# Moving one elementwise product of a selective scan from VectorE to GpSimd, and a sum from TensorE to VectorE

## The reference

```python
uc = silu(conv(u)); dtr, Bt, Ct = split(uc @ x_proj_w.T)
dt = softplus(dtr @ dt_proj_w.T + dt_proj_b)
A = -exp(A_log)
# for every token t, 256 channels, 16 states
h = exp(dt_t[..., None] * A) * h + (dt_t * u_t)[..., None] * B_t[:, None, :]
y = einsum('bdn,bn->bd', h, C_t)
```

## Time and profile before

| what | value |
|---|---|
| time, median of 3 runs | 15182.63 us (15170.1 to 15185.59) |
| profiled execution: its time, its span | 15170.1 us, 15168.0 us |
| mean granted clock of PE | 0.895 of full speed |
| busy: POOL, DVE, PE, ACT | 13633.9, 13545.8, 12942.3, 9178.0 us |

### The profile page before, as it was taken

One profiled execution on the slowest core, in us unless ns is written; L12 is line 12 of the kernel. 1 busy time (PEld: TensorE's weight loads), 2 busy tenths in 40 slices (PEclk: granted clock), 3 DMA queues, 4 the chain that ended last, 5 costly groups with the idle time before them and its releaser, 6 DMA issues.

```text
span 15168.0 us, 190881 instructions
## 1 busy us (share of the span) xinstructions
PE 12942.3 (85%) x60700; PEld 8148.5 (54%) x60700; DVE 13545.8 (89%) x9901; ACT 9178.0 (61%) x10559; POOL 13633.9 (90%) x4234
## 2 busy tenths in 40 slices
PE   7888888888888888888888888888888888888886
PEld 4555555555555555555555555555555555555554
DVE  6988998889898898988899888999989899898996
ACT  4655665656666665665566665665656666566663
POOL 6998999989999898998989998999989899898996
PEclk8998998889899888989889998889988889888997
DMA  4655555555555555555555555555555555555653
GB/s 173 231 214 209 210 217 218 216 206 211 211 220 218 209 213 207 222 219 210 209 210 216 220 212 211 211 212 219 220 205 214 207 219 219 211 211 205 222 221 131
DMA packets 582385, 3200.85 MB, mean 211 GB/s; under 512 B 65875, under 2 KB 65883, under 8 KB 319075
## 3 DMA queue, kind: packets, MB, share of 16 engines
q1 hardware_dynamic: 581346, 3187.69, 56.6%
HBM read 3107.73 MB, written 29.36 MB: 207 GB/s over the span
## 4 chain that ended last, share of the span: by engine, by line
POOL 27%; issue 25%; PE 24%; DVE 17%; ACT 5%; DMA 1%; DVEq 1%; POOLq 0%; ACTq 0%; SPq 0%
POOL ring L884 18%; PE work L1387 13%; POOL ring L867 9%; DVE ring L1375 9%; PE y_acc L1402 6%; DVE slot L1364 4%; PE slot L1387 2%; PE y_acc L1387 2%; ACT ring L1041 1%; ACT L900 1%; DMA b_rows<-cb_rows_scratch 1%; DVE du L1163 1%; ACT stack L940 1%; ACT stack L936 0%; ACT yz L966 0%
## 5 line engine op out<-in xcount | busy, mean ns | idle before, releaser
L884 POOL TENSOR_TENSOR ring<-ring,c_rows 128x2048 f32<-128x2048 f32 x2048 | 9282.8, 4536 | 997.8 <-DVE ring L1375 993.7
L1375 DVE TENSOR_TENSOR_SCAN ring<-ring,slot 128x1024 f32<-128x1024 f32 x2304 | 5263.6, 2285 | 261.6 <-ACT ring L1041 38.2
L1402 PEld LDWEIGHTS y_acc<-wk,ring 128*128 128x128 f32 x32768 | 4252.3, 155 | 1880.0 <-issue 1021.7
L1402 PE MATMUL y_acc<-wk,ring 128*128 128x128 f32 x32768 | 4762.4, 297 | 489.7 <-POOL ring L884 406.8
L867 POOL TENSOR_TENSOR ring<-du,b_rows 128x1024 f32<-128x1024 f32 x1792 | 4236.3, 2365 | 286.6 <-PE y_acc L1402 211.0
L1375 DVE TENSOR_TENSOR_SCAN ring<-slot,ring 128x1024 f32<-128x1024 f32 x1792 | 4074.2, 2274 | 192.1 <-POOL ring L867 116.5
L1041 ACT ACTIVATE slot<-dt,a_neg 128x1024 f32<-128x1024 f32 x1792 | 1997.6, 1115 | 2784.0 <-DVE ring L1375 2777.6
L1364 DVE TENSOR_TENSOR slot<-du,slot 128x1024 f32<-128x1024 f32 x2304 | 2797.4, 1214 | 271.0 <-PE slot L1387 179.7
L1041 ACT ACTIVATE ring<-dt,a_neg 128x1024 f32<-128x1024 f32 x2304 | 2600.9, 1138 | 206.5 <-PE y_acc L1402 157.3
L1387 PE MATMUL work<-h_new,fused 128*128 128x512 f32 x4096 | 2160.0, 638 | 101.7 <-ACT dt L952 53.7
L1387 PE MATMUL slot<-stack,sel 96*128 96x512 bf16 x4608 | 1540.7, 419 | 719.4 <-DVE ring L1375 639.0
(11 more groups left out here) (173 smaller groups left out, 10050.2 us busy)
## 6 DMA issues: line engine op xcount, KB each, us to landing
c_rows<-cb_rows_scratch SPq DMA_DIRECT2D x2048, 1024.0 KB, 4.7
b_rows<-cb_rows_scratch SPq DMA_DIRECT2D x1792, 512.0 KB, 5.5
x_next<-in_x SPq DMA_DIRECT2D x32, 512.0 KB, 5.4
x_new<-x_next SPq DMA_DIRECT2D x32, 512.0 KB, 6.7
h_old<-h_new SPq DMA_DIRECT2D x32, 512.0 KB, 2.9
x_old<-x_new SPq DMA_DIRECT2D x32, 512.0 KB, 6.8
out<-x_old SPq DMA_DIRECT2D x32, 512.0 KB, 2.9
cb_rows_scratch<-stack SPq DMA_DIRECT2D x128, 96.0 KB
```

Of the source, the lines that this page charges most:

```text
L884: pool.tensor_tensor(pair, pair, c_rows[:, k % CB_BUFS, :, :], ALU.mult).then_inc(prod_ready, 1)
L1375: dve.tensor_tensor_scan(slot, a, b, 0.0, MUL, ADD).then_inc(scan_done, 1)
L1402: ins = pe.matmul(chunk(out_t, j), chunk(x, j), kc("ident"), is_transpose=True, start=start and j % (BANK // P) == 0, stop=stop, skip_grou ...
```

## The change

Two things are changed. First, `timestep` is put together in another way. Ln is done in two half tiles, each from `du` into a PSUM bank; DVE adds that bank to `dt` in place (`dt_sum`, one for each half tile); POOL multiplies the whole of `dt` by `u_conv` into `du` (`dt_u`). The identity matmuls and the copy out of PSUM are gone. The waits for the first units of a pass are moved accordingly: the first decay waits for `dt_sum` on DVE, and the first DVE multiplication and the first POOL input of a pass wait for `dt_u` on POOL. Second, `KIND` is "DPDPDPDPDPDPDPDD": the counts are the same, and the two neighbouring "D" units without a "P" between them stand at the pass's end and not in its middle. The planner has costs for the new steps, and `dt_u` is due two units before the pass in place of four.

```diff
-KIND = "DPDPDPDDDPDPDPDP"
+KIND = "DPDPDPDPDPDPDPDD"
...
-    steps += [step(("dt_exp", d, h), "A"), step(("dt_ln", d, h), "A")]
+    steps += [step(("dt_exp", d, h), "A")]
     for c in range(2):
-        b = ("dt2", d, h, c)
-        steps += [step((k, d, h, c), e, b) for k, e in (("dt_add", "P"), ("dt_copy", "A"), ("dt_u", "D"))]
-    return steps
+        b = ("ln", d, h, c)
+        steps += [step(("dt_ln", d, h, c), "A", b), step(("dt_sum", d, h, c), "D", b)]
+    return steps + [step(("dt_u", d, h), "G")]
...
-             "dt_exp": 1.1, "dt_ln": 1.1, "dt_add": 1.8, "dt_copy": .6, "dt_u": .7, "turned_y": .6, "h1": .8, "relu2": .8,
+             "dt_exp": 1.06, "dt_ln": .9, "dt_sum": .7, "dt_u": 2.4, "turned_y": .6, "h1": .8, "relu2": .8,
...
-        by[("dt_u", d, 1, 1)] = 2 * NST * d + NST - 4
+        by[("dt_u", d, 1)] = 2 * NST * d + NST - 2
...
+                elif k == "dt_u":
+                    _, d, h = name
+                    ins = pool.tensor_tensor(du[:, h, :], dt[:, h, :], u_conv[:, d % 2, h, :], ALU.mult)
...
-                        pool.wait_ge(*done(base, of[("dt_u", d, h, 1)] if u > n else ("D", 0)))
+                        pool.wait_ge(*done(base, of[("dt_u", d, h)] if u > n else ("G", 0)))
...
                 elif k == "dt_ln":
-                    x = du[:, name[2], :]
-                    ins = act.activation(x, x, ACT.Ln, bias=1.0)
-                elif k == "dt_copy":
-                    ins = act.activation(half(dt[:, name[2], :], name[3]), w, ACT.Copy)
+                    _, d, h, c = name
+                    ins = act.activation(w, half(du[:, h, :], c), ACT.Ln, bias=1.0)
...
-                        act.wait_ge(*done(base, of[("dt_copy", d, h, 1)] if u else ("A", 0)))
+                        act.wait_ge(*done(base, of[("dt_sum", d, h, 1)] if u else ("D", 0)))
...
-                elif k == "dt_u":
+                elif k == "dt_sum":
                     _, d, h, c = name
-                    ins = dve.tensor_tensor(half(du[:, h, :], c), w, half(u_conv[:, d % 2, h, :], c), MUL)
+                    ins = dve.tensor_tensor(half(dt[:, h, :], c), w, half(dt[:, h, :], c), ADD)
...
-                            dve.wait_ge(*done(base, of[("dt_u", d, h, 1)] if u else ("D", 0)))
+                            dve.wait_ge(*done(base, of[("dt_u", d, h)] if u else ("G", 0)))
...
-                elif k == "dt_add":
-                    _, d, h, c = name
-                    mm(w, kc("ident"), half(dt[:, h, :], c), True, False)
-                    ins = mm(w, kc("ident"), half(du[:, h, :], c), False, True)
```

More of the change, by code:

```diff
@@ L167, in timestep @@
         rows = [("dt_cb_rows", d, c)] if (d, h) != (0, 1) else []
-        steps += [step(("dt_proj", d, h, c), "P", b, rows), step(("dt_abs", d, h, c), "A", b), step(("dt_relu", d, h, c), "A", b)]
-    steps += [step(("dt_exp", d, h), "A"), step(("dt_ln", d, h), "A")]
+        steps += [step(("dt_proj", d, h, c), "P", b, rows), step(("dt_abs", d, h, c), "A", b),
+                  step(("dt_relu", d, h, c), "A", b)]
+    steps += [step(("dt_exp", d, h), "A")]
     for c in range(2):
-        b = ("dt2", d, h, c)
-        steps += [step((k, d, h, c), e, b) for k, e in (("dt_add", "P"), ("dt_copy", "A"), ("dt_u", "D"))]
-    return steps
+        b = ("ln", d, h, c)
+        steps += [step(("dt_ln", d, h, c), "A", b), step(("dt_sum", d, h, c), "D", b)]
+    return steps + [step(("dt_u", d, h), "G")]
 def turn_y(which, f, h, after=()):
@@ L336, in comes_after @@
     if k == "b":
-        return [(("spread", u), 0)] * (u > 0 or kind == "first") + [(("dt_u", d, h, 1), 0)] * (n == 0 and u > 0)
+        return [(("spread", u), 0)] * (u > 0 or kind == "first") + [(("dt_u", d, h), 0)] * (n == 0 and u > 0)
     if k == "scan":
@@ L340, in comes_after @@
     if k == "decay":
-        first = [(("dt_copy", d, h, 1), 0)] * (n == 0 and u > 0)
+        first = [(("dt_sum", d, h, 1), 0)] * (n == 0 and u > 0)
         return first + ([(("scan", u - 2), 0)] * (u > 1) if kind_of(u) == "P" else [(("sum", u - RING), 0)] * (u >= RING))
@@ L345, in comes_after @@
     if k == "input":
-        return [(("sum", u - RING), 0)] * (u >= RING) + [(("dt_u", d, h, 1), 0)] * (n == KIND.index("P") and u > n) + rows
+        return [(("sum", u - RING), 0)] * (u >= RING) + [(("dt_u", d, h), 0)] * (n == KIND.index("P") and u > n) + rows
     if n or kind == "first" and u == 0:
@@ L385, in lay @@
     programs = unit_programs(kind)
-    by = {("result", 1): 2 * OUT_AT - 8, ("dt_u", 0, 0, 1): UNITS - 4, ("part", 0, 2, 1): UNITS - 2}
+    by = {("result", 1): 2 * OUT_AT - 8, ("dt_u", 0, 0): UNITS - 2, ("part", 0, 2, 1): UNITS - 2}
     for d in range(DIRS):
-        by[("dt_u", d, 1, 1)] = 2 * NST * d + NST - 4
+        by[("dt_u", d, 1)] = 2 * NST * d + NST - 2
         nxt = 2 * NST * d if d else UNITS
@@ L391, in lay @@
         if d:
-            by[("dt_u", d, 0, 1)] = nxt - 4
+            by[("dt_u", d, 0)] = nxt - 2
     by[("take", "before")] = 4
@@ L481, in image_plan @@
         x = [y[0] for y in s].index(("xproj", d, 0, 0))
-        s = held_back(s[:x], ("sum", 2 * NST * (d - 2) + NST + 3), ("dt_u", d - 2, 1, 1)) + s[x:] if d > 1 else s
+        s = held_back(s[:x], ("sum", 2 * NST * (d - 2) + NST + 3), ("dt_u", d - 2, 1)) + s[x:] if d > 1 else s
         y = [y[0] for y in s].index(("xproj", d, 0, 0))
@@ L496, in image_plan @@
         x = [y[0] for y in s].index(("xproj", 0, 0, 0))
-        s = held_back(s[:x], ("h1", 1), ("sum", 4 * NST + NST + 3), ("dt_u", 2, 1, 1)) \
+        s = held_back(s[:x], ("h1", 1), ("sum", 4 * NST + NST + 3), ("dt_u", 2, 1)) \
             + held_back(s[x:], pass_end(2, 1), ("dt_proj", 3, 1, 1))
@@ L953, in step @@
                 elif k == "dt_exp":
-                    x = du[:, name[2], :]
-                    ins = act.activation(x, x, ACT.Exp, scale=-1.0)
+                    h = name[2]
+                    ins = act.activation(du[:, h, :], du[:, h, :], ACT.Exp, scale=-1.0)
                 elif k == "dt_ln":
-                    x = du[:, name[2], :]
-                    ins = act.activation(x, x, ACT.Ln, bias=1.0)
-                elif k == "dt_copy":
-                    ins = act.activation(half(dt[:, name[2], :], name[3]), w, ACT.Copy)
+                    _, d, h, c = name
+                    ins = act.activation(w, half(du[:, h, :], c), ACT.Ln, bias=1.0)
                 elif k == "take":
```

## The result

The changed kernel takes 15349.42 us (median of 4 runs, 15333.85 to 15370.41) against 15176.36 us before (4 runs). The ratio is 1.0115, with a 95% interval of 1.0098 to 1.0133: 1.15% slower. The forecast was 15275 us, 0.6% slower, with a range of 15080 to 15450.

What follows compares the result with a forecast made beforehand. POOL bounds four of eight passes, DVE nearly two, PE the sixth. 9.2 - 1.2 - 1.4 + 0 - 4.5 = +2.1 us a middle image, +91 with the end images: 15275 us, 0.6% slower, whole range 15080 to 15450.

Steps and rivals of the forecast that it cites:

- POOL's added work in the full passes: Second, third, seventh and eighth pass, POOL full: nothing hides `dt_u`'s 2.30 us in each, +9.2 us an image.
- The first pass: Image start: an input fills POOL's idle time before the third product, DVE has one multiplication less ahead; -1.2 us.
- The fourth pass: Near DVE's bound: tap multiplications and their sum leave for the third pass, one half-tile multiplication comes in; -1.4 us.
- The fifth pass: Near DVE's bound: `dt_u`'s 2.3 us lie in 7.5 us of idle POOL time; 0 us, upper end +2.3.
- The sixth pass: PE's pass: identity matmuls go (4.1 us), moved steps give 0.4, `dt_u` fits in idle POOL time; -4.5 us.
- The moved steps: Sixth pass: two `dt_proj` no longer ahead of POOL's awaited sum, `post` a sum earlier; 0.4 us gained.
- ACT and the ends: ACT 1.05 us less each pass, 0 on the time; first image +18.4 us, last +9.2, lead-in 0.
- The clock: Rival: PE's granted clock in the sixth pass drops from 0.83 to 0.75, +6.8 us an image, 15480 us; 6%.
- The faster case: Rival: waits fold up, an image's idle POOL time falls from 41.6 to below 22 us; 15105 us; 25%.
- The hand-over rival: DVE-bound passes: POOL waits for `dt_sum`, then DVE for `dt_u`, 2.4 us at most in three passes; 15490 us; 6%.

Runs made afterwards that it cites:

- `u_early`: The changed kernel with `dt_u` due four units before the pass in place of two: 15361.74 us, ratio 1.0126 to the kernel before.
- `kind_only`: The kernel before with only the string KIND changed to the new one, the old time step kept: 15131.61 us, ratio 0.9975.

## Why the prediction was right, and where it was not

**POOL's added work in the full passes: right.** +9.2 us an image were forecast and +9.6 measured; with `dt_u` cut to a column, three of the four gave 1.6 to 2.2 us back. In the whole, the column kernel is 257 us under the changed one, more than the change lost, so on this plan POOL's `dt_u` is enough to make the loss. The third pass is the exception: it stayed long (56.9), and 0.8 us of its +3.1 is new idle time of POOL, so it is not shown to be `dt_u`.

**The first pass: right.** -1.2 forecast, -1.4 measured. The mean wait of the third product over the thirty images fell from 3.2 to 0.5 us, and with the old KIND on the same plan it was 3.4 again. That the sum of the pass came out is in part luck: `dt_u` by itself costs 2.0 us there (the column kernel), where the forecast had it replace an input at no cost, and the waits gave that much more.

**The fourth pass: wrong.** The step was that DVE's four tap multiplications and their sum "leave the fourth pass for the third", -1.5 us. In the stretch between POOL's eighth products they were not there to leave. DVE runs ahead of POOL, and in the kernel before the four multiplications stand in the third stretch already (third, then fourth, for L1188 alone):

```profile
7219.10:7271.90 52.80, 0.89 (x4) 0.84 0.61 229
7271.90:7336.50 64.60, 0.00 (x0) 0.89 0.50 189
```

So they do in all thirty images, and the sum in 22 of them. A plan's place was read as a place in time. DVE's busy time in the window did not fall, 60.43 us before and 60.38 after, and the pass grew by 1.4 us in the mean. POOL's `dt_u` is not the reason, for it cost nothing there. What grew is DVE's wait for PE's matmuls into the bank of the small layer, from 3.8 to 5.5 us in the mean. DVE's waits in that pass, before and then after:

```profile
DVE work L1221 <- PE work L1387: 1.9, 2, 1.4
DVE work L1217 <- PE work L1387: 1.8, 2, 1.3
```

```profile
DVE work L1219 <- PE work L1389: 5.4, 3, 2.6
DVE yz L1169 <- PE y_acc L1404: 0.7, 1, 0.7
```

The granted clock was 0.89 in that window before and 0.68 after, and some of just those matmuls ran at half speed. One pair of them before, and one after:

```profile
7292.18 1.14 PE L1387 MATMUL work<-padded,wk 40*128 40x512 f32 x2 [0.49 <-ACT dt L952]
```

```profile
7399.93 2.07 PE L1389 MATMUL work<-padded,wk 40*128 40x512 f32 x2
```

A single one took 0.67 us in the mean before and 0.87 after. So the clock can be a part of this pass's loss. It does not by itself make the pass long, since `u_early` has the same 0.68 and only 65.9 us; no run changed the clock alone, and it stays open.

**The fifth pass: wrong.** 0 was forecast and +1.8 measured. DVE's idle time in the pass stayed at 3.7 us and its busy time rose from 58.2 to 60.0: the new plan brings two half-tile statistics of the next image's norm, 0.675 us each, out of the sixth stretch into the fifth. The forecast had looked for such moved work of DVE in the fourth pass and not here. That "`dt_u`'s 2.3 us lie in idle POOL time" is not refuted: the idle time lies ahead of the instruction that `dt_u` waits for, but the fifth and sixth pass together give back only 0.4 us when `dt_u` is cut. Together they were forecast at -4.5 us and measured -4.9.

**The sixth pass: the way that was forecast, too small, and its cause shown in part.** -4.5 forecast, -6.7 measured. The stretch also lost DVE's two statistics to the fifth. PE's load put back cost 5.2 us, where 4.1 had been the term. DVE's 4.42 us of waiting for `post` and most of POOL's 6.46 us are gone; in this window POOL waited:

```profile
POOL ring L888 <- DVE ring L1377: 5.3, 2, 2.7
POOL ring L871 <- PE y_acc L1404: 1.5, 2, 1.1
POOL du L832 <- DVE dt L1165: 0.9, 1, 0.9
```

The moved steps have the remaining 1.5 us by this count, where I gave them 0.4; which of them gives it was not tried. The larger reservation is `kind_only`, which has a sixth pass of 60.8 us with all its identity additions in place. The order of the steps alone can thus give more than PE's relief, and how the 6.7 us divide between the two is not shown.

**ACT and the ends.** ACT was to lose 8.4 us an image and lost 4.6: the new plan has 1144 table loads in place of 1051, three more an image, a term that the forecast did not have. What they cost was not tried. For the first and the last image and the rest +28 us were forecast and +39 measured. The last image has its own plan and grew from 444.4 to 467.3 us, 14 more than its four full passes explain.

**The rivals.** The clock: the mean did fall, 0.895 to 0.851, but in the sixth pass, where the rival had placed it, it rose from 0.83 to 0.89, and it fell in the fourth. With PE's load put back both clock and time went up, so it is not the main cause of the loss. By the rule of the Trainium skill (TensorE: Matmul & The Clock Gate, Part 1) the clock follows PE's activity. The trace agrees in these means: PE was busy 85% before, 82% after and 84% with the load put back, at 0.895, 0.851 and 0.887. The faster case would have needed idle POOL time of 22 us; it came to 28. The hand-over rival's sign did appear, but not where it was expected. Over the whole run DVE's first multiplications of a pass waited for `dt_u`:

```profile
DVE slot L1366 <- POOL du L832: 109.8, 123, 2.5
```

That is 3.5 us a middle image, nearly all in the first, second and seventh pass; in the fourth to sixth together it is 0.2 us. POOL waited for `dt_sum` 1.2 us in the fifth pass and 0.9 in the sixth, and not the 2.4 us in three passes that this rival had priced.

**What the prediction missed altogether** is how much hangs on the order. It gave the moved pair 1.2 us in the first pass. With the plan of the changed kernel held, the old string costs 12 us an image more, though that plan was laid for the other one. And a re-plan that changes nothing but the order, and the table loads that come with it, moved the time by 2.3%.

So the closeness of the total is in part luck. +2.1 us an image were forecast and +4.7 measured. The third, fourth and fifth pass came out 0.8, 2.8 and 1.8 us above their terms, the sixth 2.2 below its own, and these errors cancel in part. What carried the sign is POOL's +9.2, which was sized well. The order by itself can move the time by more than the whole effect, and in `kind_only` a new order went the other way.

## What to carry to other kernels

Cut a loop body into stretches before pricing a move between engines: the same 2.3 us of POOL work cost 1.6 to 2.2 us in three passes in which POOL was full, nothing in the fourth, and 0.4 us in the fifth and sixth together. Look in the trace for the stretch in which a step runs, since the plan's place is not its time, and read neighbouring stretches together, since work slips over the cut. Where a planner writes the order, time a re-plan first and count what it adds (378 table loads here): its spread (2.3%) is the noise against which a change of this size is to be judged, and the parts of a change want trying on the same plan and on their own, since a plan laid for other units cost 6.8% here. Adding a P or D unit, or freeing an engine, helps only in the stretches where that engine ends the wait.

## What the runs showed of the hardware

A DVE multiplication of two SBUF tiles took 1.20 to 1.23 us where no POOL instruction was running at its start. Where one was, it was nearly always held until 1.08 us after the end of that instruction or of the next, and took 7.78 us at most (3.11 in the mean of all). A POOL product that began inside such a DVE instruction took 5.42 us in place of 4.54. With one operand in PSUM no such stretch appeared (0.67 to 0.68 us for a half tile in the kernels with `dt_sum` or the old `dt_u`). ACT's table load took 1.28 us each time. PE's granted clock, 0.842 to 0.892 in the mean over the eleven experiments, did not go with the time: 0.892 belongs to `kind_only`, the fastest that does all the work, and 0.888 to a kernel 2.3% slower than before.
